# A decoder layer on one core: GpSimd's weight-piece subtract held for the self maximum, VectorE's cross coefficients and ScalarE's gelu table moved later

## The reference, cut to what matters

```python
x = x + self_attention(layernorm(x))        # one head of 256, 2048 keys, scores = q (A^T q)^T / 16, result times the row's norm
x = x + cross_attention(layernorm(x), ctx)  # 4 heads of 64, 1601 keys, with a mask, then Wo
x = x + experts(layernorm(x))               # gate argmax of 4 experts, each 256 -> 1024 -> gelu -> 256
```

## Time and profile before

| | before |
|---|---|
| median of 3 runs | 874.06 us (873.71 to 874.42) |
| the profiled execution | 875.33 us |
| its span, first to last instruction | 873.6 us |
| PE busy (share of the span) | 767.2 us (88%) |
| DVE busy | 665.9 us (76%) |
| ACT busy | 461.4 us (53%) |
| POOL busy | 165.2 us (19%) |
| mean granted clock of PE | 0.945 |

### The profile page before, as it was taken

The page is one execution under the profiler, slowest core; times in us unless marked ns, Lnnn a source line. Parts: engine busy times, 40 slices in busy tenths (PEclk is TensorE's granted clock), DMA queues, the critical chain, the costliest instruction groups (busy, mean ns, idle before and its releaser), DMA issues. The chain is left out here.

```text
span 873.6 us, 19805 instructions
## 1 busy us (share of the span) xinstructions
PE 767.2 (88%) x6136; PEld 692.5 (79%) x6137; DVE 665.9 (76%) x1608; ACT 461.4 (53%) x930; POOL 165.2 (19%) x254
## 2 busy tenths in 40 slices
PE   3879799989999898999989899998988753999996
PEld 2769689978888797988879788887987642889996
DVE  5974647888887888888888888888888744777773
ACT  2544536665565755656565565666656530444342
POOL 3100121130312303021130302203021111222221
PEclk9999989999999999999999999999999965999999
DMA  6242251321212132131322202132149292011110
GB/s 205 68 134 68 70 197 41 117 85 48 100 36 94 57 104 100 30 100 36 100 75 80 100 30 100 36 124 100 30 133 406 88 357 65 22 39 50 36 32 15
DMA packets 51142, 80.88 MB, mean 93 GB/s; under 512 B 4894, under 2 KB 29216, under 8 KB 50976
## 3 DMA queue, kind: packets, MB, share of 16 engines
q1 hardware_dynamic: 49232, 75.63, 25.9%
q0 software_dynamic: 1872, 4.76, 1.5%
HBM read 45.60 MB, written 35.18 MB: 92 GB/s over the span
## 5 line engine op out<-in xcount | busy, mean ns | idle before, releaser
L1126 ACT ACTIVATE ps_cross<-flip 128x512 f16<-128x512 f32 (+1 forms) x256 | 124.6, 514 | 113.5 <-PE flip L845 92.3
L1351 DVE TENSOR_TENSOR ps_cross<-flip,ps_cross 128x512 f16<-128x512 f32 (+1 forms) x256 | 143.6, 582 | 10.3 <-ACT ps_cross L1126 9.9
L845 PE MATMUL flip<-ident,exp_cross 128*128 128x128 f32 (+1 forms) x832 | 132.3, 282 | 8.5 <-DVE ps_cross L1351 5.1
L834 PE MATMUL scores<-keys_cross,qt 128*128 128x402 f32 x512 | 133.3, 385 | 4.3 <-DVE xneg L1511 2.3
L1312 ACT ACTIVATE exp_cross<-exp_cross,xneg 128x1024 f32<-128x1024 f32 (+1 forms) x128 | 122.7, 960 | 15.1 <-DVE xneg L1511 15.0
L856 PE MATMUL cross_out<-vals_cross,ps_cross 128*128 128x128 f16 (+1 forms) x832 | 105.3, 228 | 28.3 <-DVE ps_cross L1351 28.2
L856 PEld LDWEIGHTS cross_out<-vals_cross,ps_cross 128*128 128x128 f16 (+1 forms) x832 | 78.5, 104 | 51.9 <-DVE ps_cross L1351 36.5
L845 PEld LDWEIGHTS flip<-ident,exp_cross 128*128 128x128 f32 (+1 forms) x832 | 96.0, 143 | 16.3 <-DVE ps_cross L1351 6.6
L722 PE MATMUL scores<-keys_self,u_tile 128*128 128x512 f32 x384 | 102.5, 404 | 6.3 <-issue 4.6
L821 PE MATMUL flip<-vals_self,ps_self 128*128 128x256 f32 x768 | 104.0, 289 | 0.0
L858 PE MATMUL cross_out<-vals_cross,ps_cross 128*128 128x64 f16 (+1 forms) x832 | 98.2, 198 | 0.0
(11 more groups left out here) (197 smaller groups left out, 1240.8 us busy)
## 6 DMA issues: line engine op xcount, KB each, us to landing
rows_dram<-pads SPq DMA_DIRECT2D x17, 520.0 KB, 3.9
w_piece<-W SPq DMA_DIRECT2D x32, 256.0 KB, 2.9
w_dram<-w_high SPq DMA_DIRECT2D x32, 256.0 KB, 2.3
w_dram<-w_piece SPq DMA_DIRECT2D x32, 256.0 KB, 2.7
w1s<-w_dram SPq DMA_DIRECT2D x8, 1024.0 KB, 11.3
w2s<-w_dram SPq DMA_DIRECT2D x8, 1024.0 KB, 10.8
u_dram<-u_out SPq DMA_DIRECT2D x4, 1024.0 KB, 5.9
u_tile<-u_dram SPq DMA_DIRECT2D x16, 256.0 KB, 2.8
```

The lines of the kernel that those rows point to most:

```text
L834: mm = pe.matmul(scores[:, n, 0:KB], qt[:, h, :], keys_cross[:, part, h, n * KB:(n + 1) * KB], start=(part == 0), stop=(part == 1))
L845: tr = pe.transpose(flip[0:rows, bank(use), n * P:(n + 1) * P], exp_cross[:, h % 2, m * P:m * P + rows], ident[:, :])
L1126: return act.activation(out, in_, ACT.Copy, **kw)
L1351: return dve.tensor_tensor(out, full, hi, ALU.subtract)
```

## The change

GpSimd's subtract of the weight piece also waits for `self_max` of its stage. VectorE's three coefficient instructions go from before `cross_lo(3, 0)` to behind `self_lo(1)`. ScalarE's gelu on one column, and with it the table load, goes from the start of stage 17 to behind `cross_hi(3, 3)`.

```diff
@@ GpSimd, body(j, k), part a
                 pool.wait_ge(piece_hi, j + 1)
+                pool.wait_ge(self_max, j + 1)
                 pool.tensor_tensor(w_piece[:, :, :], w_piece[:, :, :].bitcast(F32), w_high[:, :, :].bitcast(F32),
                                    ALU.subtract).then_inc(piece_lo, 1)
@@ ScalarE, body(j, k)
             a, b, c = k < T, 1 <= k <= T, k >= 2
-            if k == T + 1:
-
-                act.activation(barrier[:, 1:2], ident[:, 0:1], ACT.Gelu).then_inc(gelu_table, 1)
             if c:
                 cross_hi(j, k, 2, 2)
...
                 cross_hi(j, k, 3, 3)
+            if k == T + 1:
+
+                act.activation(barrier[:, 1:2], ident[:, 0:1], ACT.Gelu).then_inc(gelu_table, 1)
             if a:
                 self_hi(j, k, 1)
@@ VectorE, body(j, k)
                 dve.tensor_reduce(sneg[:, 0:1], smax[:, :], AX.X, ALU.max, negate=True).then_inc(self_max, 1)
             if c:
-
+                cross_lo(j, k, 3, 0)
+                cross_lo(j, k, 3, 1)
+                cross_lo(j, k, 3, 2)
+            if b:
+                cross_max(j, k, 0, 0)
+            if a:
+                self_lo(j, k, 0)
+            if c:
+                cross_lo(j, k, 3, 3)
+            if a:
+                self_lo(j, k, 1)
+            if c:
                 dve.wait_ge(cross_exp_ready, 8 * (j - 1))
                 dve.tensor_tensor(xcoef[:, 2, :], xden[:, 0, :], xden[:, 1, :], ALU.add).then_inc(o_step, 1)
                 dve.wait_ge(o_step, 3 * (j - 1) - 2)
                 dve.reciprocal(xcoef[:, 0, :], xcoef[:, 2, :]).then_inc(o_step, 1)
                 dve.wait_ge(o_step, 3 * (j - 1) - 1)
                 dve.tensor_scalar(xcoef[:, 1, :], xcoef[:, 0, :], v_scale[:, 1:2], None, ALU.mult).then_inc(o_step, 1)
-                cross_lo(j, k, 3, 0)
-                cross_lo(j, k, 3, 1)
-                cross_lo(j, k, 3, 2)
-            if b:
-                cross_max(j, k, 0, 0)
-            if a:
-                self_lo(j, k, 0)
-            if c:
-                cross_lo(j, k, 3, 3)
-            if a:
-                self_lo(j, k, 1)
             if b:
                 cross_max(j, k, 0, 1)
```

More of the change, by code:

```diff
@@ L1540, in body @@
             if c:
[L1542 to L1547, removed]
                 cross_lo(j, k, 3, 0)
@@ L1558, in body @@
                 self_lo(j, k, 1)
+            if c:
+                dve.wait_ge(cross_exp_ready, 8 * (j - 1))
+                dve.tensor_tensor(xcoef[:, 2, :], xden[:, 0, :], xden[:, 1, :], ALU.add).then_inc(o_step, 1)
+                dve.wait_ge(o_step, 3 * (j - 1) - 2)
+                dve.reciprocal(xcoef[:, 0, :], xcoef[:, 2, :]).then_inc(o_step, 1)
+                dve.wait_ge(o_step, 3 * (j - 1) - 1)
+                dve.tensor_scalar(xcoef[:, 1, :], xcoef[:, 0, :], v_scale[:, 1:2], None, ALU.mult).then_inc(o_step, 1)
             if b:
```

## The result

| | before | after |
|---|---|---|
| median of 4 runs each | 873.88 us | 826.55 us (825.48 to 828.52) |
| the profiled execution | 875.33 us | 825.48 us |
| its span | 873.6 us | 823.7 us |
| PE busy (share of the span) | 767.2 us (88%) | 747.4 us (91%) |
| DVE busy | 665.9 us (76%) | 628.6 us (76%) |

The ratio of the times is 0.947, with an interval of [0.944, 0.949]. The forecast was 828.7 us, the range 826 to 838.

The account below looks back on a forecast made before the run. TensorE, the busiest engine, was held by VectorE's coefficient multiply, which ended with GpSimd's subtract. Savings 42.7 + 3.5 - 1.4 - 0.6 - 0.2 + 1.4 = 45.4 us gave 828.7 us, range 826 to 838.

Parts of the forecast that it names:

- The cause: Loop stages: VectorE's coefficient multiply ends only with GpSimd's subtract; TensorE waits 2.13 us, then loses 1.7 us of clock.
- The loop: 12 iterations at stage 2's 33.66 us plus 0.39 at the branch: 408.6 in place of 451.33 us, 42.7 saved.
- Stage 15: Stage 15 falls from 37.19 us to stage 2's 33.66, saving 3.5 us.
- The lateness: Coefficients behind `self_lo(1)` delay VectorE 0.6 us; slack leaves 0.1 lost in 14 stages, 1.4 us; bounds 0 to 8.4.
- Rival B: VectorE becomes the pace; its 0.6 us lateness could reach TensorE fully, 7 us more, 836 us; chance 0.10.
- A: TensorE's clock doesn't come back, perhaps through the piece's writes: 1.7 us kept in 13 stages, 851 us; chance 0.05.
- C: GpSimd's subtract also holds VectorE's 128x512 low parts to float16: 0.7 us in 13 stages, 838 us; chance 0.08.
- D: Something else releases VectorE's subtract of (3, 0), so nothing is saved at the wait: 882 us; chance 0.02.
- E: VectorE's coefficients run into GpSimd at their new place too; the wait stays, near 865 us; chance 0.03.
- The held subtract: GpSimd's wait for the maximum acts only in stages 1 and 2; cost 0, at most 3.2 us once.
- The tail: Stages 16 and 17: later coefficients lose 0.6 and 0.2 us; ScalarE's late gelu table saves 1.4 us.
- The executions: Profiled execution lies 1.3 us above the 874.06 median; same difference taken after the change: 829.9 and 828.7 us.

Follow-up runs that it names:

- e2_hold_only: The kernel before, with only GpSimd's subtract of the weight piece also waiting for the self maximum; 873.91 us, ratio 1.000.
- e4_hold_for_coef: The kernel before, with GpSimd's subtract waiting until its stage's three coefficient instructions are out, VectorE's order and early table kept; 827.33 us, ratio 0.945.
- e5_mult_late: The kernel before, with only the multiply of the three coefficient instructions moved behind the second self low part; 826.94 us, ratio 0.948.
- e10_mult_gelu: The kernel before, with only the coefficients' multiply moved late and the gelu table loaded late, no GpSimd hold; 826.10 us, ratio 0.944.
- e9_written_out: The kernel with the multiply and the gelu table late, but stages 3 to 14 written out instead of the hardware loop; 814.56 us, ratio 0.932.
- e6_idle2: The changed kernel plus an unused VectorE maximum over 2700 constants ahead of the first low part in the 12 loop stages; 868.4 us, ratio 0.994.
- e3_gelu_only: The kernel before, with only the gelu table loaded later; 871.93 us, ratio 0.998.
- the second measurement: The changed kernel measured again, unaltered, beside three other kernels on one chip; 829.96 us, ratio 0.949.

## Why the prediction was right, point by point

**The cause.** The blocked multiply, and the stage of 33.66 us that the trace already held as a model, carried the forecast. The lock was made (e2_hold_only), avoided from GpSimd's side (e4_hold_for_coef) and by moving one instruction (e5_mult_late); all three moved the stage as the reading said, but for the clock's part, which e2_hold_only's stage 2 didn't pay.

**The loop.** Forecast 12 x (33.66 + 0.39) + 12 x 0.1 = 409.8, measured 411.02 us. The sum is close because two of its terms are wrong against each other, and that they cancel is luck. The turn of the loop costs not 0.39 us, which is only the idle time in front of the branch, but (408.06 - 397.35) / 12 = 0.89 us (e10_mult_gelu against e9_written_out). And a later stage is not 33.66 us long but 33.11, or 33.20 in stage 15 of the changed kernel. Stage 2, the model, only looks some 0.5 us longer (33.68 in e9_written_out too): the mark that begins it lies early in TensorE's work. In e9_written_out TensorE transposes `xn` 2.14 us behind the mark at 145.01, but 1.55 us behind the next mark, at 178.69:

```profile
147.15 0.38 PE L870 MATMUL flip<-ident,xn 128*128 128x128 f32 x2
...
180.24 0.38 PE L870 MATMUL flip<-ident,xn 128*128 128x128 f32 x2
```

From one to the other are 33.09 us, a stage like the later ones. The prediction's own check hinted at it: 37.72 - 2.13 - 1.70 = 33.9 still contains the 0.39 us at the branch, so what is left is 33.5, below 33.66, while the text read the 0.39 as most of a difference of 0.2. And stage 13 of the kernel before was a better model, a loop stage at full clock: 36.13 - 2.13 = 34.00 us, which is what e5_mult_late and e10_mult_gelu measured.

**Stage 15.** Forecast 3.5 us less, measured 4.0, for the same reason.

**The lateness.** Forecast 0.1 us in each stage. Measured: 0.10 in stage 2, and 34.25 - 34.12 = 0.13 against e4_hold_for_coef, whose coefficients are early; 0.24 against e10_mult_gelu (34.01), where only the multiply is late. So the term was sized too small, by up to 1.7 us in the loop, within its stated bounds. TensorE's fourth transpose of self exponentials starts at 400.18, 0.06 us behind the end of `self_lo(2)` at 400.12, so the slack of the earlier trace rows is used up, as the step said. Rival B had the right place, and a small part of its price.

**Rivals A and C.** A fell by the clock of 1.00 in all loops that lack the wait, and by e6_idle2, where the slow stretch follows the idle time without the lock. C fell by the pair at 394.24. The rule cited from the Trainium skill, page "SBUF — State Buffer", section "Who interferes with whom", holds here for 128x512 low parts to float16 too.

**D and E** did not come: the first low part starts 0.1 us behind the maximum, and the multiply is short in all 16 stages.

**The held subtract.** Forecast nothing, measured nothing in the time; its one effect alone is to make stage 2 of the kernel before 1.65 us worse. In the changed kernel, its place in stages 1 and 2 hurts nobody since the coefficients are gone from there.

**The tail.** Forecast 1.4 saved and 0.8 lost, 0.6 less; measured 2.8 us less in stages 16 and 17. Stage 16 did not lose its 0.6: `cross_max(0, 0)` waited 1.58 us for the mask bias in place of 2.45. The table is worth about 1.3 us by all executions (see e3_gelu_only), close to the 1.4 of the forecast. From the routing of stage 16 to the last, the kernel before took 22.47 us, 0.8 to 1.0 more than the four other executions with the early table; that part of the 2.8 belongs to the one execution.

**Not forecast:** 2.56 us up to the end of stage 1, where nothing changed but GpSimd's hold. In the thirteen profiled executions of this study this mark lies between 144.1 and 148.7 us, with and without each edit, so it belongs to the execution and not to the change. Without it, the 49.9 us of span would be 47.3; that this is also the difference of the medians is chance, since the two medians of the changed kernel are themselves 3.4 us apart.

**The executions.** The prediction took the profiled execution to lie as far above the median before as after. It lay 1.3 us above the median of 874.06 before, and 1.1 below the median after; the sum of 45.4 us was off by 4.5 for the profiled pair, by 1.9 for the medians, and by 1.4 the other way for the second measurement (873.98 - 829.96 = 44.0 us).

## What to carry to other kernels

When a tiny instruction shows two durations, 0.23 and 2.32 us here, look at what ends with it on the neighbouring engine. Here GpSimd held VectorE for a whole instruction; that VectorE holds GpSimd was not seen (the subtract took 2.34 to 2.40 us in all runs). Delaying GpSimd by 0.4 us was a cure, and so was moving the one instruction away. Look in the trace for a stage that by chance lacks the trouble: it prices the cure better than a sum of waits, and in this case its length also held the clock's part. But check that the marks cut both stages at the same place of the busiest engine's work. And a written-out pipeline can be worth more than the idle time shown at a loop's branch: 0.89 us for 0.39 shown.

## What the runs showed of the hardware that was not expected

An idle time of TensorE of 1.60 us cost only itself (clock 1.00). One of 1.95 or 2.13 us mostly cost 1.6 to 1.7 us more, through 3.7 us at a mean clock of 0.54 to 0.56, but not always: in 4 of 39 stages with waits of 2.05 us and more the clock stayed at 1.00. The same work in a hardware loop took 0.89 us more per turn than written out: by the windows of the 12 stages, 0.52 of it is time in which TensorE isn't busy (6.50 us in e10_mult_gelu, 0.22 in e9_written_out), of which 0.39 stands at the branch, and 0.37 is busy time (401.56 against 397.13 us), though the instructions are the same. Followed by TensorE's rows over one stage (from 311.16 us in e9_written_out, from 316.63 in e10_mult_gelu), the two keep step within 0.1 us for 25 us, then the loop falls back by 0.3 us until the small product of line 886, and by 0.46 us between that and the next scores, at the branch. What holds it up ahead of the branch was not tried.
